# First transform of a four-layer spectral network on four 64x64 TensorE tiles, two chunks at a time

## The reference

```python
xs = jnp.fft.rfft2(xf32, axes=(1, 2)).reshape(B, H, Wm, 8, 48)
o1r = relu(xr @ w1[0] - xi @ w1[1] + b1[0])
o1i = relu(xi @ w1[0] + xr @ w1[1] + b1[1])
o2r = o1r @ w2[0] - o1i @ w2[1] + b2[0]
o2i = o1i @ w2[0] + o1r @ w2[1] + b2[1]
out_c = softshrink(o2r, 0.01) + 1j * softshrink(o2i, 0.01)
return jnp.fft.irfft2(out_c, s=(H, W), axes=(1, 2)) + x
```

## Time and profile before

| | |
|---|---|
| time, median of 3 runs | 2103.13 us (2093.58 to 2103.71) |
| profiled execution | 2097.06 us |
| its span, first to last instruction | 2095.1 us |
| PE matmul busy | 1975.4 us, 94% |
| PE weight loads busy | 1669.1 us, 80% |
| VectorE / ScalarE / GpSimd busy | 1162.5 / 892.3 / 442.8 us |
| mean granted TensorE clock | 0.984 |

### The profile page before, as it was taken

One profiled execution on the slowest core, in us unless ns is written; L12 is line 12 of the kernel. 1 busy time (PEld: TensorE's weight loads), 2 busy tenths in 40 slices (PEclk: granted clock), 3 DMA queues, 4 the chain that ended last, 5 costly groups with the idle time before them and its releaser, 6 DMA issues.

```text
span 2095.1 us, 68654 instructions
## 1 busy us (share of the span) xinstructions
PE 1975.4 (94%) x31104; PEld 1669.1 (80%) x31104; DVE 1162.5 (55%) x2462; ACT 892.3 (43%) x1470; POOL 442.8 (21%) x425
## 2 busy tenths in 40 slices
PE   5999995799998999999999999999899999999996
PEld 4787773687776999999999999999788778887884
DVE  2686888876945333333333333332466666666675
ACT  2544444455553333333333333333354444444542
POOL 3212013975821000000000000000321211220300
PEclk9999997899999999999999999999999999999999
DMA  9425637407444111111111111114903555457314
GB/s 162 98 44 86 116 59 136 71 4 128 116 91 109 31 31 31 30 30 30 30 30 30 30 30 30 30 31 72 142 3 74 86 97 103 73 82 127 63 33 92
DMA packets 299697, 141.05 MB, mean 67 GB/s; under 512 B 275632, under 2 KB 298032, under 8 KB 299440
## 3 DMA queue, kind: packets, MB, share of 16 engines
q1 hardware_dynamic: 299440, 137.11, 36.1%
HBM read 74.17 MB, written 62.91 MB: 65 GB/s over the span
## 4 chain that ended last, share of the span: by engine, by line
PE 79%; DVE 11%; issue 3%; DMA 2%; POOL 2%; SPq 1%; ACT 1%; POOLq 0%; DVEq 0%; ACTq 0%
PE ps L617 19%; PE ps L602 19%; PE ps L453 7%; PE ps L516 7%; PE ps L467 7%; PE ps L437 6%; PE ps L531 6%; PE ps L484 6%; DVE u L836 4%; DVE st L873 2%; DVE xs L861 1%; DVE clamp L830 1%; PE ps L495 1%; PE ps L587 1%; POOL xs L1080 1%
## 5 line engine op out<-in xcount | busy, mean ns | idle before, releaser
L983 DVE TENSOR_TENSOR gl<-g,gh 128x512 fp32r<-128x512 f32 x192 | 156.8, 817 | 476.4 <-ACT gh L781 476.4
L836 DVE TENSOR_TENSOR u<-ps,clamp 64x192 f32<-64x192 f32 (+1 forms) x864 | 378.5, 438 | 27.7
L778 ACT ACTIVATE g<-ps,colp 128x512 f32<-128x512 f32 x192 | 132.3, 689 | 529.3 <-PE ps L602 529.3
L453 PEld LDWEIGHTS ps<-const,z 128*48 128x48 f32 x8384 | 274.9, 124 | 100.5 <-issue 92.0
L453 PE MATMUL ps<-const,z 128*48 128x64 f32 (+1 forms) x8384 | 274.0, 217 | 7.2 <-issue 5.1
L437 PE MATMUL ps<-const,xn 128*64 128x64 f32 x6144 | 221.5, 226 | 44.4 <-POOL xn L1070 22.8
L830 DVE TENSOR_SCALAR clamp<-ps 128x384 f32<-128x384 f32 (+1 forms) x216 | 112.7, 522 | 271.1 <-PE ps L484 271.1
L617 PE MATMUL ps<-w2h,gh 128*128 128x384 f32 x768 | 261.9, 341 | 0.0
L617 PE MATMUL ps<-w2h,gl 128*128 128x384 f32 x768 | 258.6, 337 | 0.0
L617 PE MATMUL ps<-w2l,gh 128*128 128x384 f32 x768 | 257.5, 335 | 0.0
L467 PE MATMUL ps<-zf,w 112*64 112x512 f32 (+2 forms) x992 | 249.3, 567 | 0.1
(11 more groups left out here) (69 smaller groups left out, 2473.5 us busy)
## 6 DMA issues: line engine op xcount, KB each, us to landing
after<-xs SPq DMA_DIRECT2D x96, 384.0 KB, 5.4
xs<-after SPq DMA_DIRECT2D x94, 384.0 KB, 8.8
after<-om SPq DMA_DIRECT2D x32, 384.0 KB, 4.3
out<-xs SPq DMA_DIRECT2D x32, 384.0 KB, 5.5
xm<-after SPq DMA_DIRECT2D x30, 384.0 KB, 6.3
xs<-in_x SPq DMA_DIRECT2D x24, 384.0 KB, 8.5
wstage<-in_spectral SPq DMA_DIRECT2D x16, 210.0 KB, 7.4
xs<-in_x SPq DMA_DIRECT2D x4, 768.0 KB, 11.8
```

Source lines behind the costliest of these rows:

```text
L453: mm = pe.matmul(ps[a * SIDE:a * SIDE + BLOCK, F2_BANK, n * L.kh:(n + 1) * L.kh], z[:, g % 2, slot, :], basis(col + a * SIDE, L.kh), start ...
L836: dve.tensor_tensor(u[to, g % 2, :, start + b:start + size:BATCH], whole, limited, ALU.subtract).then_inc(u_ready, 1)
L983: dve.tensor_tensor(gl[:, n % 4, :], g[:, n % 2, :], gh[:, n % 4, :], ALU.subtract).then_inc(g_low, 1)
```

## The change

f1 now works on two chunks ("twin") at a time, 16 channels, with 32 matmuls of 64 rows by 64 columns. The block-diagonal basis is gone: the 64x64 basis stands twice, once for each image's partitions. The stationary operand is one channel of one image; image b goes to bank b, and even and odd channels go to the upper and lower half of the partitions. So the four quarters of the array (two halves of rows, two of columns) take turns. The number of matmuls per channel stays at two.

A twin's result lies crosswise, so it is copied to z in four pieces of 64 partitions by 512 elements (j: channel parity, a: real or imaginary) instead of two copies of 128 by 512. ScalarE does two pieces in the twin's slot behind zf, the third in the next slot ahead of h, the fourth between h and zf. A twin needs both banks, so it waits for all pieces of the twin before. Twins stand in slots 0, 3 and 6 (norm: 0, 1, 2).

At the head of each segment the three twins of its first block use banks (0, 1), (6, 7), (0, 1), and VectorE does two of the four pieces. In the norm segment it does so behind the centring of three chunks.

GpSimd prepares weights at the end of an odd block. SyncE issues their load right behind the unit's stores, ahead of the wait for them and of the loads of x.

```diff
-C_D1, C_D2, C_D2A, C_D2B, C_SIGN = [P * n for n in range(5)]
+C_D1 = 0
+C_D2, C_D2A, C_D2B, C_SIGN = [SPAN + P * n for n in range(4)]
...
-        self.f1_at = [0, 1, 3, 5, 7, 8] if self.full else [0, 0, 1, 2, 2, 3]
+        self.f1_at = [0, 3, 6] if self.full else [0, 1, 2]
+        self.centre_at = [0, 0, 1, 2, 2, 3]
...
+        def spectrum_piece(g, k, j, a, banks):
+
+            first = 2 * k * CHAN + j
+            to = z[a * SIDE:(a + 1) * SIDE, g % 2, :, first:first + 2 * CHAN - 1:2]
+            data = ps[j * SIDE:(j + 1) * SIDE, banks[0]:banks[1] + 1, :]
+            return (to.rearrange("p (k b) c -> p k b c", b=BATCH),
+                    data.rearrange("p b (c a k) -> p a k b c", a=2, k=HALF)[:, a])
...
+                load_weights(first + 2)
                 for unit in range(first, last):
-                    if unit + 2 < UNITS:
-                        load_weights(unit + 2)
...
                     store_unit(unit)
+                    if unit + 3 < UNITS and unit != 2 * PAIRS - 1:
+                        load_weights(unit + 3)
...
                 for c in range(CHAN):
-                    for a in range(2):
-                        mm = pe.matmul(ps[a * SIDE:(a + 1) * SIDE, F1_BANKS[n % 2], c * SPAN:(c + 1) * SPAN],
-                                       xn[:, n % RING, c, :], basis(C_D1 + a * SPAN, SPAN), start=True, stop=True)
+                    slot, first = (chunk - 1 + c // (CHAN // 2)) % RING, c % (CHAN // 2) * 2
+                    for b in range(BATCH):
+                        rows = slice(b * SIDE, (b + 1) * SIDE)
+                        for j in range(2):
+                            mm = pe.matmul(ps[j * SIDE:(j + 1) * SIDE, banks[b], c * SPAN:(c + 1) * SPAN],
+                                           xn[rows, slot, first + j, :], const[rows, C_D1:C_D1 + SPAN],
+                                           start=True, stop=True)
...
+                        late = at_slot(L.f1_at, t - 1) if g + 1 < last else []
+                        ahead = at_slot(L.f1_at, t) if g + 1 < last else []
+                        behind = at_slot(L.f5_at, t) if g > first else []
+                        for k in late:
+                            f1(g + 1, k, PIECES[2:3])
                         if t:
                             m1(g, t - 1)
                         elif g > first:
                             m1(g - 1, layer_of(g - 1).n - 1)
+                        for k in late:
+                            f1(g + 1, k, PIECES[3:4])
                         f2(g, t)
...
+            def f1(g, k):
+
+                dve.wait_ge(f1_done, TWINS * g + k + 1)
+                for j, a in PIECES[2:4]:
+                    to, data = spectrum_piece(g, k, j, a, LEAD_BANKS[k])
+                    dve.tensor_scalar(to, data, layer_of(g).forward, None, ALU.mult).then_inc(z_shared, 1)
...
-                        if k == 2 and g % 2 and g > first + 1 and g + 1 < 4 * BLOCKS:
-                            weights((g + 1) // 2)
+                    if g % 2 and g > first + 1 and g + 1 < 4 * BLOCKS:
+                        weights((g + 1) // 2)
...
-    d1 = np.einsum("wak,bd->bwakd", col, np.eye(BATCH)).reshape(P, 2 * SPAN)
+    d1 = np.tile(col.reshape(SIDE, SPAN), (BATCH, 1))
```

More of the change, by code:

```diff
@@ L32 @@
 CHUNKS = BLOCK // CHAN
+TWINS = CHUNKS // 2
+PIECES = ((0, 0), (0, 1), (1, 1), (1, 0))
 ROWCHUNK = 8
@@ L123, in rows_at, with leads, z_before, z_shared_before @@
     return [(g - 2, t + 1)] if t < ROWCHUNKS - 1 else []
+def leads(g):
+    return any(g == first for first, _ in SEGMENTS)
+def z_before(g, k=0):
+    return sum(TWINS * (2 if leads(n) else 4) for n in range(g)) + k * (2 if leads(g) else 4)
+def z_shared_before(g, k=0):
+    return sum(2 * TWINS for n in range(g) if leads(n)) + (2 * k if leads(g) else 0)
 def at_slot(order, t):
@@ L425, in f1 @@
                 L = layer_of(g)
-                n = CHUNKS * g + k
+                chunk = CHUNKS * g + 2 * k + 1
                 if L.norm and g == BLOCKS:
@@ L429, in f1 @@
                 elif L.norm:
[L430 removed]
+                    pe.wait_ge(xn_ready, chunk - CHUNKS * (BLOCKS + 1) + 1)
                 else:
[L432 to L438 removed]
+                    pe.wait_ge(xt_ready, chunk + 1 - (CHUNKS * BLOCKS if L.index > 1 else 0))
+                free = z_before(g, k - 1 if leads(g) and k == TWINS - 1 else k)
+                shared = z_shared_before(g, k - 1 if k == TWINS - 1 else 0)
+                if free:
+                    pe.wait_ge(z_ready, free)
+                if shared:
+                    pe.wait_ge(z_shared, shared)
+                banks = LEAD_BANKS[k] if leads(g) else F1_BANKS
+                if leads(g) and g and k == 1:
+                    pe.wait_ge(res_ready, ROWCHUNKS * g)
+                for c in range(CHAN):
+                    slot, first = (chunk - 1 + c // (CHAN // 2)) % RING, c % (CHAN // 2) * 2
[5 more added lines that the diff above has]
+                                           start=True, stop=True)
                 mm.then_inc(f1_done, 1)
@@ L536, in spectral @@
             def spectral(first, last):
-                for k in range(CHUNKS):
+                for k in range(TWINS):
                     f1(first, k)
@@ L730, in spectral @@
                         normalise_row(r)
-                for k in range(CHUNKS):
-                    f1(first, k)
+                for k in range(TWINS):
+                    f1(first, k, PIECES[0:2])
                 for g in range(first, last):
@@ L739, in spectral @@
                             m1(g - 1, layer_of(g - 1).n - 1)
+                        for k in late:
+                            f1(g + 1, k, PIECES[3:4])
                         f2(g, t)
-                        ahead = at_slot(L.f1_at, t) if g + 1 < last else []
-                        behind = at_slot(L.f5_at, t) if g > first else []
-                        for k in ahead[0:1]:
-                            f1(g + 1, k)
-                        for k in behind[0:1]:
-                            f5(g - 1, k)
-                        for k in ahead[1:]:
-                            f1(g + 1, k)
-                        for k in behind[1:]:
+                        for k in ahead:
+                            f1(g + 1, k, PIECES[0:2])
+                        for k in behind:
                             f5(g - 1, k)
@@ L911, in spectral @@
                         centre(n)
+                for k in range(TWINS):
+                    f1(first, k)
                 for g in range(first, last):
@@ L915, in spectral @@
                         rows = [r for r in rows_at(g, t) if r[0] >= first]
-                        ahead = [CHUNKS * (g + 1 - first) + k + AHEAD for k in at_slot(L.f1_at, t)] if norm else []
+                        ahead = [CHUNKS * (g + 1 - first) + k + AHEAD for k in at_slot(L.centre_at, t)] if norm else []
                         ahead = [n for n in ahead if n < CHUNKS * (last - first)]
```

29 lines of the change are left out of this document (14 added, 15 removed).

## The result

The changed kernel takes 2126.12 us (median of 4 runs, 2123.25 to 2131.13) against 2101.36 us for the kernel before (4 runs, 2093.58 to 2103.71): a ratio of 1.0127, 95% interval 1.0093 to 1.0161. It is slower by 25 us. The profiled execution took 2123.25 us, its span is 2121.5 us, 26.4 more than the span of before.

A forecast was written before the change was run, and what follows sets the result against it. PE, its matmuls busy 94% of the span, was taken as the bound. The terms summed to 81T - 93.4, +1.4 us at T = 1.17; on the median of 2103.13 us the forecast was 2104, range 2076 to 2155.

The forecast's parts named there:

- each switch empties the array: Rival, 20%: both ends of each of some 90 f1 bursts cost 0.25 us, +22 us, 2125.
- T: PE's time for one f1 twin, burst plus two switches: forecast 0.93 + 2 x 0.12 = 1.17 us.
- The burst, 0.93: A twin's 64 f1 records take 0.93 us on PE if the four quarters run side by side; 1.86 at most.
- Issuing at 22.2 ns: Rival, 8%: PE starts f1 records no faster than every 22.2 ns, a twin takes 1.66 us, +41, 2144.
- row halves without overlap: Rival, 12%: the array's row halves gain nothing in f1, a twin takes at least 1.86 us, +57, 2160 or more.
- The switch, 0.12: PE going between 128-row and 64-row matmuls, twice per twin: 0.12 us each, between 0 and 0.25.
- the free switch: Rival, 22%: going between 128-row and 64-row matmuls costs PE nothing, a twin takes 0.93 us, -18, 2085.
- The lost cover: Full blocks: slots losing f1 become waits for VectorE's u, slot 2 waits for zf; 33.16 + 3T against 36.48 us.
- The norm slots, 3T - 4.66: Change per norm block, seven blocks: six f1 of 0.93 go, three twins come, waits add 0.9 us.
- The head of the norm segment, +5: Once, where VectorE is the bound: six pieces of 0.6 us and GpSimd's later keep add 5 us, ends 3 and 12.
- The weights, -2.5: The new place of weight loads ends late GpSimd chunks that hold PE: -2.5 us, ends 0 and -5.
- The pieces' length: ScalarE's copies to z: 0.60 us each, upper end 0.69, which would add about 0.4 us per block, 8 in all.

The follow-up runs named there:

- paced: The changed kernel with the four parts of a unit's load of x issued two slots apart (one in the norm layer): 2117.43 us, ratio 1.0103.

## Why the prediction was right or wrong

The time lies in the range (2076 to 2155) and on the side that had the larger chance, but it is not the forecast of 2104. It is about a microsecond from the rival "each switch empties the array" (2125), and that agreement is a coincidence of the sum: the switch cost 0.155 us, not the rival's 0.25, and other terms were too low. At the measured T the recorded sum gives +7 us instead of +1.4. The head adds 6.4, the norm blocks 5 and the rest of the full block 1.8; of the 6 that are left up to 3.7 are longer stalls (20.8 against 17.1).

**The burst, 0.93: right.** 0.94 measured. Issuing at 22.2 ns and row halves without overlap fall: records follow each other every 14.6 ns. By the floor of about 25 ns between the starts of matmuls that the Trainium skill gives (TensorE: Matmul & The Clock Gate, the section "Wait — 56ns, not 53.3ns?") it would have been an estimated 1.6 us; the trace disagrees.

**The switch, 0.12: a little low.** 0.155, shown twice, by slots (5.24 - 4.00) and by doubling it (+0.30). Over 81 twins that is +5.7 us. The rule of TensorEngine Tiling (Array Packing), Key Properties, in the Trainium skill, that a change of mode drains the engine, agrees in kind: at 1591.34 and 1592.43 the new mode's first load holds back 0.15 us, where it otherwise starts with the old burst's last record. The trace adds the price, 0.155 us, between the free switch and the 0.25 us of the rival.

**The lost cover: right.** Slots 7 and 8 were forecast at 3.69 (3.68, 3.67), slot 1 at 2.81 (2.83), 4 and 5 at 4.00 (4.00), slot 2 at 4.48 (4.63) with 0.65 of wait for zf (0.54). The sum of the block, 33.16 + 3T, gives 36.88 at the measured T; 36.99 measured. The run with other slots confirms it, the same work in 1.1 us a block less, and corrects its weight: 0.34 of this is cover, and 0.75 the zf wait in slot 2.

**The norm slots, 3T - 4.66: too low.** At T = 1.24 it gives -0.9 a block, -6.6 in all. A block without a stall takes 29.65 us against 29.88, -0.23, which is -1.6 in seven; the segment measured +2.4, with two stalls of 4.3 and 2.9 us (paced, -1.3, also with stalls). The two slots with two f5 were forecast with 0.3 of wait for v each; there is 0.39 more in each, f1 waiting for the fourth piece of the twin in the slot before, behind h. I had counted the pieces' time ahead of v and not their own consumer, the next twin.

**The head of the norm segment, +5: the term that was off by most.** +11.4 (+12.9 paced), at the upper end that the prediction kept (12). The six pieces cost 4.3 us of VectorE, not the 3.6 counted; but the third twin needs banks 0 and 1, the last to free them are VectorE's pieces, and these stood behind three centrings of 3.6 us. What counts is the place in the queue, not the length. The lower clock behind that wait, some 2 us, stood in no term.

**The weights, -2.5: right for the kernel before (-3.6), wrong as a term of this change.** It was priced by the waits that it would end, and not by those that twins would have added: 59 us.

**The pieces' length** is 641 ns on average, in the middle of 600 to 690, and ScalarE's busy time 1012 us (about 1000 forecast). Halving the pieces gave 15 us, more than the 8 at stake in their length: their number and places count.

**Not settled.** Layer 0 lost 3.5 us (5.9 paced), 3 of it in one block of the paced run (37.8 against 34.5). There ScalarE waits 1.7 us for the token network's weights (L770, `wraw`) with the late pieces and h behind it, PE's m2 waits 1.6 us for h, and the clock is at 0.50 for 3 us behind that; how much of it is the change's, one execution does not tell. That the stalls are PE's own instruction fetches is not shown. Most of them fall in full DMA traffic, and the two longest of the changed kernel beside a packet of instructions; but in the same trace PE stops for 1.5 us at 266.9 and for 1.9 at 1883.3 with the DMA engines under 10% busy. With the loads spread they shrink in layers 0, 2 and 3, while one of 2 to 4 us stays in the norm segment.

**Is there a version that beats both?** Twins in slots 1, 4 and 7 of the full layers, single chunks in the norm layer, moved weights and paced loads: ratio 0.9929. The same without twins stands at 0.9967. So four quarters are worth 0.4%, 6 us, in these places and with single chunks in the norm layer. That is less than 0.6 us a block would give (7 us in blocks 18 to 29 of layers 2 and 3 alone). There the two profiled executions differ by 3.2 us: 5.0 are gained in these blocks, where small stalls take 2 of the 7 back, and 2.3 lost in the first block of layer 2 (33.7 against 31.4), in which m2 stops for 2.3 us in the middle of its burst. In layer 0 the two are equal (251.2 and 251.3).

## What to carry to other kernels

When work leaves an engine that is 94% busy, ask first which waits it covered: here six bursts shrank by a third, and the whole became 25 us slower; other places in the order gave 18 of them back. When two pieces of work are joined into one, every producer must now have both ready and every consumer must release both; look in each queue for what stands between the two (the weights' transfer, three centrings, h), and price that, not the length of the copies. A wait of 12 us of the busiest engine can also cost clock behind it, so look at the granted clock there. And measure kernels with stalls in their trace against paced ones before explaining a few microseconds.

## What was unexpected of the hardware

- PE started 64-row, 64-column float32 records every 14.6 ns (64 in 0.94 us), twice as fast as 128-row ones (29 ns), and paid 0.155 us for each change between 64 and 128 rows.
- PE stopped in the middle of bursts for 0.5 to 4.5 us with its operands ready, mostly while 8 loads of 384 KB were under way. Spreading four pairs of loads two slots apart took 15 us off one kernel (1.0006 to 0.9929), 3 off another (0.9983 to 0.9967) and 5 off a third (1.0127 to 1.0103), at the same bytes.
- At the head of the norm segment, with PE mostly idle, the granted clock stood at 0.50 until about 395 us (to 373 before), and f2's 64 records took 2.77 us instead of 1.61.
